# One layer of a graph network: TensorE's increments moved from the last matmul of a group to a drain

## The chip, the core and the metric

The kernel runs on one core of one Trainium2 chip (trn2). A core has five engines with an instruction stream each: PE (TensorE, matmuls), DVE (VectorE), ACT (ScalarE), POOL (GpSimd) and SP (SyncE), and 16 DMA engines that carry what these issue. Engines order themselves by semaphores: an instruction adds one to a semaphore when it is done (`then_inc`), and another engine waits until the semaphore has reached a number (`wait_ge`). The metric is the device time of one execution in microseconds (us); less is better.

## What is computed

6250 nodes have 128 features each, and 206250 edges (sorted by their target node) have 50 features each. In the names of the reference, with x the input and h its normalised copy:

```
h   = relu(layernorm(x))
W   = silu(edge_attr @ fw1 + fb1) @ fw2 + fb2        # a filter for every edge
t   = silu(h @ aw1 + ab1) @ aw2 + ab2                # a row for every node
agg = segment_sum(W * t[src], dst)                   # sums over the edges of a target
out = x + h + silu(agg @ ow1 + ob1) @ ow2 + ob2
```

All of it is in float32, but for the bias fb2, which is split in three bf16 parts that are added by a matmul.

## The kernel before, in words

**First stage.** The rows t of all nodes are computed in seven chunks and written to a table in HBM (`node_table`).

**Edge stage.** The padded edges are cut into 202 pairs of groups; a pair is 1024 edges, a group 512. 196 pairs are "main" pairs and take t[src] from the table; 6 "early" pairs compute it from gathered rows of x. For main pair q the engines do this:
- POOL (L281 to L288) issues 8 indirect DMAs, each of which gathers 128 rows of the table into one of five buffers `xg`. Before the first four of a pair, and again before the last four, it waits on `msg_done`: the buffer must have been consumed by the pair five places before.
- PE has one stream. In `pair(q)` (L769) it does `hidden(q + 1)`: two matmuls of the 50 edge features with fw1, one for each group (`hidden_of`, L738; written to `hid_ps`); then, for each of the two groups, `filters_of` (L745): four matmuls with fw2 and one that adds fb2, into one of four banks `fil_ps`; then `window(q - 2)` (`window_of`, L752): two matmuls that scatter row sums into a window of 64 target nodes.
- ACT does silu on the hidden layer (L353, sets `hid_done`) and multiplies the messages by a mask, eight instructions (L357).
- DVE multiplies filters with gathered rows (`msg`, L595, sets `msg_done`), builds the one-hot matrices (L563, L567), sums rows (L571, sets `red_done`) and adds the window of pair q - 3 to `agg` (L576).

A float32 matmul of the program is two instructions MATMUL and two LDWEIGHTS in the trace, a bf16 one is one of each. So `hidden_of` is 4 + 4 instructions, `filters_of` 9 + 9 and `window_of` 4 + 4; a pair has 26 MATMUL and 26 LDWEIGHTS. Records of some L749 and L742 matmuls are missing in the trace; their weight loads are there.

**Who waits for PE.** `hidden_of` ends with an increment of `hid_sum` (ACT's silu waits for it, and SP's next load of edge features), `filters_of` with one of `fil_done` (DVE's product waits for it, and ACT before it overwrites `hid`), `window_of` with one of `win_done` (DVE's addition). The same three helpers serve the early pairs with semaphores of their own. Transposes (L680) and the layers of the nodes (L686, L691, L698, L795) have their own increments on matmuls.

**Order.** `main_part` (L61) is written out by hand: main pairs come in runs of 32, 32, 32, 32, 32, 20, 8 and 8 (`RUNS`). Between runs stand an early pair (five times, one more before the first run) and the output of nodes whose sums are complete (`output`, L818 on PE). POOL's stream knows no runs: it gathers on until the five buffers are full.

Of the kernel before, what the change touches and what calls it, by code (L numbers as in the profile page):

```python
# [28 lines left out]
WIN = 64  # L29
# [57 lines left out]
def gnn_layer(nc, x, src_t, dst_t, attr_t, fw1, fb1, fw2, fb2, aw1, ab1, aw2, ab2, ow1, ob1, ow2, ob2, out):  # L87
# [8 lines left out]
    with ExitStack() as ctx:  # L96
        def sb(name, shape, dt=f32):
            return ctx.enter_context(nc.sbuf_tensor(name, shape, dt))
# [11 lines left out]
        fw1_s = sb("fw1_s", [P, F])  # L110
# [31 lines left out]
        sums = sb("sums", [P, SETS, 2, F])  # L142
        onehot = sb("onehot", [P, SETS, 2, WIN])
# [25 lines left out]
        hid_ps, fil_ps, sum_ps = bank[0:2], bank[2:6], bank[6:8]  # L169
# [507 lines left out]
        def _(pe):  # L677
# [60 lines left out]
            def hidden_of(to, features, signal):  # L738

                for half in range(2):  # L740
                    at = slice(HALF * half, HALF * half + NG)
                    i = pe.matmul(to[half], fw1_s[at, :], features[at, :], start=True, stop=True)  # L742
                i.then_inc(signal, 1)

            def filters_of(to, b, signal):  # L745
                for j in range(TPG):
                    pe.matmul(to[:, j * P:(j + 1) * P], hid[:, b, j * P:(j + 1) * P], w["fw2_s"][:, :],  # L747
                              start=(j == 0), stop=False)
                pe.matmul(to, ones_b[:, :], fb2_rows[:, :, :].rearrange("p j f -> p (j f)"), start=False,  # L749
                          stop=True).then_inc(signal, 1)  # L750

            def window_of(s, b, signal):  # L752
                for m in range(2):
                    i = pe.matmul(sum_ps[b][:, 0:WIN], sums[:, s, m, :], onehot[:, s, m, :], start=(m == 0), stop=(m == 1))  # L754
                i.then_inc(signal, 1)

            def hidden(q):
                if q % PART == 0:
                    pe.wait_ge(attr_in[q // PART % 2], (q // PART // 2 + 1) * 32)
                pe.wait_ge(hid_done, run(2 * q + 1, 2))  # L760
                at = q % (2 * PART) * GC
                hidden_of(hid_ps, attr[:, at:at + GC], hid_sum)

            def window(q):
                pe.wait_ge(win_added, run(q, 2))
                pe.wait_ge(red_done, run(q))
                window_of(q % SETS, q % 2, win_done)

            def pair(q, s, last):  # L769
                if s == 0:  # L770
                    hidden(q)
                if not last:
                    hidden(q + 1)
                for h in range(2):
                    g = 2 * q + h
                    pe.wait_ge(msg_done, run(g, 4))
                    pe.wait_ge(hid_done, run(g))
                    filters_of(fil_ps[g % 4], g % 4, fil_done)
                if s >= 2:
                    window(q - 2)  # L780
                if last:
                    window(q - 1)
                    window(q)

            def early(r, mlp):
# [10 lines left out]

                pe.wait_ge(e_attr_in, r * 32 + 32)
                hidden_of(e_hid_ps, e_attr, e_hid_sum)
                transposed(0)
                first_layer(0)  # L800
                for h in range(2):
                    e = 2 * r + h
                    pe.wait_ge(e_msg_done, run(e, 1))
                    pe.wait_ge(e_hid_done, run(e))
                    filters_of(e_fil_ps, h, e_fil_done)
                    if h == 0:
                        transposed(1)
                    pe.wait_ge(s_mid, run(mlp + h))
                    pe.wait_ge(s_res, run(mlp + h, 1))
                    layer2(e_l2_ps, TPG, w["aw2_s"][:, :], s_l2)  # L810
                    if h == 0:
                        first_layer(1)
                pe.wait_ge(e_oh_done, r + 1)
                pe.wait_ge(e_red_done, r + 1)
                window_of(0, 0, e_win_done)
                pe.wait_ge(e_added, r + 1)

# [65 lines left out]
```

## Time and profile before

| | |
|---|---|
| time, median of 2 runs | 2673.2 us (2668.84 to 2677.57) |
| the profiled execution | 2694.56 us, of it the span from first to last instruction 2692.7 us |
| busy share of the span | POOL 57%, PE 47%, DVE 45%, PE weight loads 33%, ACT 30% |
| mean granted TensorE clock | 0.669 of full speed |
| DMA | mean 60 GB/s; the gathers (queue q0) 106.01 MB, 15.0% of the 16 engines' time |

A row of a group of instructions gives line, engine and operation, the tiles written and read, and how many (x); then busy time in all, the mean of one in ns, and the time its engine stood idle just before them with what ended that. A row of a timeline begins with start and duration in us; in brackets stands the idle time before it and what ended it. "issue" means that nothing the profile shows was waited for, "remote" that the releaser was not found.

### The profile page before, as it was taken

The numbers are of one execution on the slowest core, as the hardware profiler recorded it, in microseconds if no ns is written. First come the engines' busy times: TensorE is split into PE (matmuls) and PEld (weight loads), VectorE is DVE, ScalarE is ACT, GpSimd is POOL, SyncE is SP. The second block draws the span as 40 slices with busy tenths as digits, with TensorE's granted clock in tenths as the row PEclk, the third lists the DMA queues.
The fourth block names the chain that finished last, engine by engine and source line by source line (L and its number), as shares of the span: only waits on it lengthen the run. The fifth ranks groups of instructions, "written<-read, shape, count | busy, mean of one in ns | idle before, by whom it ended". The sixth has DMA issues, their size and how long they took to land.

```text
span 2692.7 us, 19814 instructions
## 1 busy us (share of the span) xinstructions
PE 1275.5 (47%) x5623; PEld 894.4 (33%) x5727; DVE 1208.9 (45%) x1637; ACT 798.9 (30%) x2154; POOL 1538.6 (57%) x1623
## 2 busy tenths in 40 slices
PE   1344554544544545445445454545444545553544
PEld 1233332332433433323333332333333323332333
DVE  2624444434445443544443444544454443445345
ACT  1222332323323223323332332323232322322232
POOL 7346666626666635666645666654666663666552
PEclk8666666667666656776667677666767667666766
DMA  4212222202222212222212222211222221222210
GB/s 128 93 29 69 56 71 61 68 27 67 62 57 72 59 36 58 71 57 73 57 44 54 65 61 57 73 50 48 58 69 57 72 56 43 54 72 56 55 50 21
DMA packets 64445, 160.54 MB, mean 60 GB/s; under 512 B 28144, under 2 KB 30036, under 8 KB 59436
## 3 DMA queue, kind: packets, MB, share of 16 engines
q0 software_dynamic: 51712, 106.01, 15.0%
q1 hardware_dynamic: 10176, 49.70, 6.9%
q10 hardware_dynamic: 2448, 3.54, 0.4%
q8 instruction: 48, 0.79, 0.1%
q14 instruction: 61, 0.50, 0.1%
HBM read 152.72 MB, written 6.42 MB: 59 GB/s over the span
## 4 chain that ended last, share of the span: by engine, by line
another core or an unknown queue 37%; DVE 23%; PE 20%; issue 14%; DVEq 3%; ACT 3%; DMA 0%; SPq 0%; ACTq 0%
DVE sums L571 12%; PE banks L747 7%; DVE msg L595 6%; PE banks L742 5%; DVEq L574 3%; PE banks L754 2%; PE banks L749 2%; ACT msg L357 1%; DVE onehot L567 1%; PE banks L686 1%; PE banks L698 1%; PE banks L691 1%; DVE agg L576 1%; PE banks L795 1%
## 5 line engine op out<-in xcount | busy, mean ns | idle before, releaser
L286 POOL DMA_INDIRECT xg<-node_table,src x1568 | 1491.3, 951 | 1091.8 <-DVE msg L595 599.6
L357 ACT ACTIVATE msg<-msg,other 128x128 f32<-128x128 f32 x1616 | 494.5, 388 | 1392.5 <-DVE msg L595 1315.5
L595 DVE TENSOR_TENSOR msg<-banks,xg 128x512 f32<-128x512 f32 x392 | 269.5, 688 | 1187.2 <-remote 1033.4
L571 DVE TENSOR_REDUCE sums<-msg 128x128 f32<-128x1024 f32 x404 | 753.1, 1904 | 10.4 <-ACT msg L357 3.5
L747 PE MATMUL banks<-fw_s,hid 128*128 128x128 f32 x3232 | 628.2, 342 | 206.1 <-issue 205.6
L747 PEld LDWEIGHTS banks<-fw_s,hid 128*128 128x128 f32 x3232 | 563.3, 247 | 435.8 <-issue 391.7
L754 PE MATMUL banks<-onehot,sums 128*128 128x64 f32 x808 | 168.4, 347 | 854.8 <-DVE agg L576 471.4
L754 PEld LDWEIGHTS banks<-onehot,sums 128*128 128x128 f32 x808 | 152.2, 258 | 908.4 <-issue 885.7
L742 PE MATMUL banks<-attr,fw_s 50*128 50x512 f32 x784 | 303.9, 862 | 140.0 <-ACT hid L353 116.0
L353 ACT ACTIVATE hid<-banks,cols 128x512 f32<-128x512 f32 x392 | 244.5, 672 | 204.5 <-remote 128.4
L749 PE MATMUL banks<-fb_rows,ones_b 128*128 128x512 bf16 x300 | 139.4, 465 | 33.6 <-issue 33.6
L742 PEld LDWEIGHTS banks<-attr,fw_s 50*128 50x128 f32 x784 | 76.6, 239 | 174.6 <-ACT hid L353 131.2
L329 ACT ACTIVATE mid<-banks,cols 128x512 f32<-128x512 f32 (+4 forms) x28 | 22.9, 817 | 168.6 <-PE banks L686 74.3
L576 DVE TENSOR_TENSOR agg<-agg,banks 128x64 f32 x202 | 42.8, 212 | 52.4 <-issue 22.2
L749 PEld LDWEIGHTS banks<-fb_rows,ones_b 128*128 128x128 bf16 x404 | 47.8, 118 | 55.2 <-issue 55.0
L567 DVE SCALAR_TENSOR_TENSOR onehot<-iota,ends,onehot 128x64 f32<-128x64 f32 x202 | 55.6, 275 | 0.0
L275 POOL DMA_INDIRECT e_x<-in_x,src x48 | 46.0, 959 | 16.1 <-issue 14.3
L691 PE MATMUL banks<-aw_s,mid 128*128 128x128 f32 x194 | 30.0, 310 | 36.0 <-ACT mid L329 36.0
L795 PE MATMUL banks<-hT,aw_s 128*128 128x512 f32 x24 | 22.6, 1043 | 48.0 <-DVE hT L615 47.2
L563 DVE TENSOR_TENSOR onehot<-iota,ends 128x64 f32<-128x64 f32 x202 | 43.7, 216 | 0.0
L691 PEld LDWEIGHTS banks<-aw_s,mid 128*128 128x128 f32 x194 | 28.3, 224 | 38.6 <-ACT mid L329 38.0
L622 DVE TENSOR_TENSOR e_x<-banks,rows 128x512 f32<-128x512 f32 x12 | 8.3, 692 | 72.7 <-PE banks L691 54.7
(89 smaller groups left out, 315.6 us busy)
## 6 DMA issues: line engine op xcount, KB each, us to landing
attr<-in_attr SPq DMA_DIRECT2D x98, 400.0 KB
xg<-node_table,src POOLq DMA_INDIRECT x1568
xs<-in_x SPq DMA_DIRECT2D x5, 448.0 KB
node_table<-res SPq DMA_DIRECT2D x5, 448.0 KB, 2.5
out<-res ACTq DMA_DIRECT2D x5, 448.0 KB, 2.5
e_attr<-in_attr SPq DMA_DIRECT2D x12, 100.0 KB
msg<-in_dst SPq DMA_DIRECT2D x1, 808.0 KB
src<-in_src SPq DMA_DIRECT2D x1, 784.0 KB
```

Source lines behind the costliest of these rows:

```text
L286: pool.indirect_dma_start(xg[:, q % XG, j, :], None, table[:, :], bass.IndirectOffsetOnAxis(ap=src[:, q * L + j:q * L + j + 1], axis=0))\
L353: act.activation(hid[:, g % 4, :], hid_ps[h], ACT.Silu, bias=cols[:, 0:1]).then_inc(hid_done, 1)
L357: i = act.activation(msg[:, b, 1, j, :], msg[:, b, 0, j, :], ACT.Identity, scale=other[:, tiles + j:tiles + j + 1])
L567: dve.scalar_tensor_tensor(out=onehot[:, b, 1, :], in0=iota[:, 0:WIN], scalar=ends[:, 1, q:q + 1], in1=onehot[:, b, 0, :], op0=ALU.is_equa ...
L571: dve.reduce_sum(sums[:, s, m, :], msg[:, b, m, :, :].rearrange("p j f -> p f j"), AX.X).then_inc(signal, 1)
L574: base = dve.value_load(base_i[0:1, q:q + 1], min_val=0, max_val=N_NODES)
L595: dve.tensor_tensor(msg[:, q % 2, 0, tiles, :].rearrange("p j f -> p (j f)"), fil_ps[(2 * q + h) % 4], xg[:, q % XG, tiles, :].rearrange(" ...
L691: i = pe.matmul(to[:, j * P:(j + 1) * P], mid[:, j * P:(j + 1) * P], weights, start=True, stop=True)
L742: i = pe.matmul(to[half], fw1_s[at, :], features[at, :], start=True, stop=True)
L747: pe.matmul(to[:, j * P:(j + 1) * P], hid[:, b, j * P:(j + 1) * P], w["fw2_s"][:, :], start=(j == 0), stop=False)
L749: pe.matmul(to, ones_b[:, :], fb2_rows[:, :, :].rearrange("p j f -> p (j f)"), start=False, stop=True).then_inc(signal, 1)
L754: i = pe.matmul(sum_ps[b][:, 0:WIN], sums[:, s, m, :], onehot[:, s, m, :], start=(m == 0), stop=(m == 1))
```

## The change

At the end of `hidden_of`, `filters_of` and `window_of` the last matmul no longer carries the increment. A `drain` is issued behind it on PE, and the drain carries the increment. The matmuls, their order, all waits and all numbers waited for stay as they are. Increments of the transposes and of the node layers stay on their matmuls.

```
-                    i = pe.matmul(to[half], fw1_s[at, :], features[at, :], start=True, stop=True)
-                i.then_inc(signal, 1)
+                    pe.matmul(to[half], fw1_s[at, :], features[at, :], start=True, stop=True)
+                pe.drain().then_inc(signal, 1)
...
                 pe.matmul(to, ones_b[:, :], fb2_rows[:, :, :].rearrange("p j f -> p (j f)"), start=False,
-                          stop=True).then_inc(signal, 1)
+                          stop=True)
+                pe.drain().then_inc(signal, 1)
...
-                    i = pe.matmul(sum_ps[b][:, 0:WIN], sums[:, s, m, :], onehot[:, s, m, :], start=(m == 0), stop=(m == 1))
-                i.then_inc(signal, 1)
+                    pe.matmul(sum_ps[b][:, 0:WIN], sums[:, s, m, :], onehot[:, s, m, :], start=(m == 0), stop=(m == 1))
+                pe.drain().then_inc(signal, 1)
```

## Rows read from the trace of the kernel before

**Rows 1.** The page's costliest groups of instructions, over the whole span.

```profile
L286 POOL DMA_INDIRECT xg<-node_table,src x1568 | 1491.3, 951 | 1091.8 <-DVE msg L595 599.6
...
L595 DVE TENSOR_TENSOR msg<-banks,xg 128x512 f32<-128x512 f32 x392 | 269.5, 688 | 1187.2 <-remote 1033.4
...
L747 PE MATMUL banks<-fw_s,hid 128*128 128x128 f32 x3232 | 628.2, 342 | 206.1 <-issue 205.6
L747 PEld LDWEIGHTS banks<-fw_s,hid 128*128 128x128 f32 x3232 | 563.3, 247 | 435.8 <-issue 391.7
```

**Rows 2.** Who waited for whom, whole span: us in total, times, longest us.

```profile
DVE msg L595 <- remote: 1033.4, 142, 12.5
...
POOL xg L286 <- DVE msg L595: 599.6, 98, 42.4
```

**Rows 3.** The same for POOL alone, 606 to 1000 us (second run of 32 pairs).

```profile
POOL xg L286 <- DVE msg L595: 53.4, 13, 5.0
```

**Rows 4.** Timeline inside that run, 843 to 873 us.

```profile
843.99 0.68 DVE L595 TENSOR_TENSOR msg<-banks,xg 128x512 f32<-128x512 f32 x1
...
845.27 2.08 PE L747 MATMUL banks<-fw_s,hid 128*128 128x128 f32 x8
...
847.56 1.09 PE L747 MATMUL banks<-fw_s,hid 128*128 128x128 f32 x8
...
850.25 1.16 PE L747 MATMUL banks<-fw_s,hid 128*128 128x128 f32 x8
...
851.47 0.50 PE L747 MATMUL banks<-fw_s,hid 128*128 128x128 f32 x3
...
852.96 0.27 PE L747 MATMUL banks<-fw_s,hid 128*128 128x128 f32 x1 [1.00 <-issue]
...
854.47 0.69 DVE L595 TENSOR_TENSOR msg<-banks,xg 128x512 f32<-128x512 f32 x1 [5.75 <-issue]
...
862.48 0.95 POOL L286 DMA_INDIRECT xg<-node_table,src  x1 [0.30 <-issue]
867.15 0.69 DVE L595 TENSOR_TENSOR msg<-banks,xg 128x512 f32<-128x512 f32 x1 [11.80 <-remote]
...
868.11 0.95 POOL L286 DMA_INDIRECT xg<-node_table,src  x1 [4.68 <-DVE msg L595]
...
871.75 0.69 DVE L595 TENSOR_TENSOR msg<-banks,xg 128x512 f32<-128x512 f32 x1
```

**Rows 5.** Engines by stretch: length, busy us (instructions) of each, clock, DMA share, GB/s.

```profile
192.37:198.54 6.17, 5.16 (x32) 2.90 (x30) 5.34 (x7) 4.68 (x14) 4.73 (x5) 1.00 0.16 43
...
838.72:868.11 29.39, 13.80 (x65) 9.79 (x65) 11.74 (x16) 7.43 (x21) 18.92 (x20) 0.67 0.31 79
605.00:961.00 356.00, 176.22 (x786) 124.61 (x800) 168.09 (x215) 111.07 (x308) 230.60 (x245) 0.66 0.25 64
```

**Rows 6.** Timeline after POOL's restart at 192.37 us.

```profile
200.24 1.27 ACT L353 ACTIVATE hid<-banks,cols 128x512 f32<-128x512 f32 x2 [0.34 <-remote]
...
204.55 0.27 PE L747 MATMUL banks<-fw_s,hid 128*128 128x128 f32 x1 [0.51 <-issue]
```

**Rows 7.** Timeline between the second and third run, 960 to 1018 us.

```profile
960.84 0.69 DVE L595 TENSOR_TENSOR msg<-banks,xg 128x512 f32<-128x512 f32 x1
...
968.28 2.08 PE L742 MATMUL banks<-e_attr,fw_s 50*128 50x512 f32 x4
...
975.26 1.27 ACT L383 ACTIVATE hid<-banks,cols 128x512 f32<-128x512 f32 x2 [9.72 <-remote]
...
1009.66 1.13 PE L742 MATMUL banks<-attr,fw_s 50*128 50x512 f32 x4 [1.18 <-DVE res L642]
1010.84 1.27 ACT L353 ACTIVATE hid<-banks,cols 128x512 f32<-128x512 f32 x2 [5.91 <-PE banks L742]
...
1016.77 0.69 DVE L595 TENSOR_TENSOR msg<-banks,xg 128x512 f32<-128x512 f32 x1 [7.03 <-remote]
...
1017.73 0.94 POOL L286 DMA_INDIRECT xg<-node_table,src  x1 [42.06 <-DVE msg L595]
```

## The prediction

> **What bounds the kernel now.** I read the groups of instructions first. The reader should see that no engine is busy throughout, and that POOL, the busiest, issues 1568 gathers [rows 1]. A gather costs 0.95 us plus 0.30 us between two [rows 4], 1.25 us in all, so a pair costs 10 us and 196 pairs 1960 us: the floor of the edge stage. The waits say what comes on top: POOL stood 599.6 us until a product of DVE freed a buffer [rows 2]. In a run of 32 pairs it waited 53.4 us in 13 pauses [rows 3], 1.67 us a pair, so 327 us over 196 pairs; the remaining 273 us are the eight long pauses between runs, one of which was 42.06 us [rows 7].
>
> The timeline shows what stops DVE in a run. After the product at 843.99, PE issues four groups of filters (845.27, 847.56, 850.25, 851.47) and DVE makes its products in that order: the one at 854.47 uses the first, the one at 867.15 the second, whose matmuls were over by 849 [rows 4]. DVE waited 11.80 us. It was not for gathered rows: POOL had filled all five buffers and could only stop (last gather issued at 862.48), so the oldest of forty had been issued 50 us before. It was for `fil_done`: PE's increment came 18 us after its matmul. Between the products at 854.47 and 867.15 lie 12.68 us, and one filter group is 18 instructions: 0.70 us each. And PE's own issue, eight matmuls in 1.1 us until then, falls to such steps from 852.96. So instructions of PE leave it slowly, increments come out in their order, and once the queue behind is full, issue slows too. The release comes when POOL stops: 3.7 us after its last gather ended at 863.43 comes the product at 867.15, POOL goes on at 868.11, and the next product (871.75) waits for nothing [rows 4]. With gathers under way an early pair's first layer, done by 970.36, was seen by ACT at 975.26; without gathers the same matmuls ended at 1010.79 and ACT began at 1010.84 [rows 7]. This is a loop: PE held, DVE starved, POOL full, POOL stops, PE released.
>
> **How much gets through.** After a restart 32 + 30 instructions of PE go by before the first late one (ACT at 200.24 [rows 5, 6]); its issue has visibly slowed by 204.55 [rows 6]. A cycle from restart to restart (838.72 to 868.11) has 65 + 65 = 130 instructions of PE and 20 gathers, 2.5 pairs [rows 5]. My balance: 62 pass at once (6.2 us); then one per 0.70 us until the release at 28.4 us, 31 more; 130 - 93 = 37 stand in the queue when it opens. For n pairs a cycle, 52n = 62 + (10n - 2.5) / 0.70 + 37, which gives n = 2.5.
>
> **The change, part by part.** Each of 202 first layers, 404 filter groups and 202 windows gets a drain: 808 more instructions on PE, 4 a pair. Removed is nothing but the increment on the matmul.
>
> (a) The drain itself. No row has one. Below I bound it by nothing, above by the 0.70 us steps of rows 4. I take 0.25 us: a weight load of L747 takes 247 ns [rows 1] and no longer overlaps the matmul before it. That is nearest, because the drain's sure effect is that break. In a run that is 1.0 us a pair on PE, which is busy 176.22 of 356 us, 5.5 us of 11.1 a pair [rows 5], so it is hidden by the wait for gathers; without that cover it would cost 196 us. Between runs the chain goes through PE: two windows, then with an early pair its first layer, two filters and window, then first layers and filters of the next run, about nine drains in five gaps and five in three, 60 x 0.25 = +15 us. At 0 us it is 0, at 0.70 us +42.
>
> (b) The wait that the drain adds. Behind it on PE stand the next group's weight loads, which now don't enter the queue until the drain is through; for them wait ACT (silu), DVE (product, window) and so POOL. If a drain waits until the instructions before it have come out, the 37 that now stand in the queue at the release can't be there; at most one group of 18 can. With 56 instructions a pair: 56n = 62 + (10n - 2.5) / 0.70 + 18 gives n = 1.83. A pause costs 1.67 x 2.5 = 4.2 us a cycle; over 1.83 pairs that is 2.29 us a pair, +0.62, x 196 = **+121 us**. Ends: nothing queued, n = 1.40, 3.0 us a pair, +260 us; the whole queue kept, n = 2.28, +0.17, +33 us; below zero only if a drain's increment escapes the hold, which is a rival. I take the middle one, since a group of 18 is what rows 4 show coming out in one piece.
>
> The Trainium skill ("PSUM — Partial Sum Buffer", section "Engine vs sequencer instructions") says that the increment belongs on the matmul, and that a drain waits for the engine to go fully idle. That speaks against this change: it is (b); no row here shows a drain beside matmuls.
>
> (c) The semaphores' other waiters, SP for feature loads among them, see the same order and numbers; SP loads four pairs ahead, so a shift of under 1 us is nothing.
>
> Sum against the profiled execution: 2692.7 + 15 + 121 = 2829, plus the 1.9 around the span, 2831. Its median stands 0.8% below the profiled time (2673.2 / 2694.56 = 0.992), so the forecast is **2808, say 2810 us**. That the unprofiled time is so near also says that the pauses are not made by profiling alone: without them it would be 300 us less.
>
> **Rival 1: the drain's increment escapes (faster).** If the drain waits only for the array and its increment is not queued behind the instructions, and issue no longer clogs, POOL never pauses in a run: 327 less 0.3 for each of some 90 pauses, -300 us. Between runs 56 us pass from last to first product [rows 7], and with empty buffers POOL fills 50 of them: 42.06 becomes some 7, five times -35; two short pauses of together some 34 us vanish. 2692.7 - 300 - 175 - 34 + 15 = 2199, timed 2180. The increments left on matmuls would still be held between runs (4.9 us for one at 975.26), at three or four a gap up to +100: 2280. If only every second pause goes, 2540. For it: the increments are what DVE waits for. Against: PE's issue slows to the same steps for matmuls that carry no increment (852.96), and that a drain can't mend. It decides from the point where a pause comes less often than every four pairs.
> The Trainium skill ("Perfetto Trace Analysis", section "Sequencer-only Instruction (DRAIN, etc)") has a drain's increment pushed by the sequencer and not by the engine, which would be this rival.
>
> **Rival 2: prompt increments, same limit (no change).** The increments escape, but PE's instructions still pass at 0.70 us while gathers run: whole queue kept, +33, drains +15, and an early pair's first layer and filters come sooner, some 7 us in five gaps, -35. 2692.7 + 13 = 2706, timed 2690 (2650 to 2725).
>
> **Rival 3: nothing stays queued and drains are slow.** 2692.7 + 260 + 42 = 2995, timed 2970; if DVE, which then has no filters ready, falls behind after each release by one group's 1.1 to 2.1 us [rows 4], per 1.4 pairs, +150: 3120.
>
> **Chances.** The forecast's case (2730 to 2930) 0.38; rival 3 0.16; rival 2 0.22, of which 0.20 inside 2%; rival 1 0.24. Within 2% (2620 to 2727, about what a measurement tells from no change) 0.20, slower 0.56, faster 0.24. The likeliest case's own range is 2730 to 2930. For 8 in 10 I leave out the full form of rival 1 (0.16) and the tail over 3030 (0.04): 2560 to 3030.
>
> **What would show it.** (b) right: POOL's pauses in a run come every 16 gathers or less instead of 20 and their sum over a run of 32 is above 70 us; filters of at most one group are issued between a held product and its release; the wait of DVE on "remote" stays. (a) right: drains of 0.1 to 0.3 us between runs, the long pauses some 2 us longer each. Wrong, and rival 1 right: few pauses in runs, DVE waiting on gathers that landed just before, long pauses of 7 to 25 us. Rival 2 right: increments within 1 us of the matmul's end and still pauses of 4 us every 2 to 2.5 pairs, with PE issuing in 0.70 us steps ahead of them. If the 0.70 us steps are gone altogether, my account of the queue is wrong.

## The result: slower, and the profile after

The changed kernel takes **2867.48 us** (median of 2 runs, 2859.3 to 2875.66) against 2673.2: a ratio of **1.0727, with a 95% interval of 1.0575 to 1.0878**. The forecast was 2810 us, slower: right in direction, 57 us too low. The profiled execution took 2875.66 us, its span 2873.9 us, 181.2 us more than before, at a mean granted clock of 0.636 (before 0.669).

The page's groups of instructions after the change, in the order of [rows 1]; each helper of the change has moved one line for every line put in, and the product of filters is still L747:

```profile
L286 POOL DMA_INDIRECT xg<-node_table,src x1568 | 1487.6, 949 | 1278.4 <-DVE msg L595 790.8
...
L595 DVE TENSOR_TENSOR msg<-banks,xg 128x512 f32<-128x512 f32 x392 | 270.7, 691 | 1229.2 <-PEq L751 1204.7
...
L747 PE MATMUL banks<-fw_s,hid 128*128 128x128 f32 x3232 | 698.8, 385 | 483.2 <-issue 478.8
```

And who waited for whom, as in [rows 2], over the whole span (us in total, times, longest us), then for POOL alone in the run of 32 pairs that answers to [rows 3] (606 to 1050 us):

```profile
DVE msg L595 <- PEq L751: 1204.7, 324, 11.8
...
POOL xg L286 <- DVE msg L595: 790.8, 107, 48.7
```

```profile
POOL xg L286 <- DVE msg L595: 130.1, 18, 44.7
```

The reader sees the loss in one number. POOL does the same 1488 us of work, but waits 790.8 us for a product of DVE where it waited 599.6 [rows 2]: +191.2 us beside a span that is 181.2 us longer. DVE waits on `PEq L751`, the drain of the filters, 1204.7 us, where the wait of [rows 2] had no releaser's name. In the timelines, eight pauses between runs are over 14 us and add up to 283.4 us (before: eight, 273.9 us); 99 pauses inside runs hold the other 507.4 us (before: 90 pauses, 325.7 us).

One cycle from restart to restart of POOL, the counterpart of [rows 4] and of the window 838.72:868.11 in [rows 5]:

```profile
878.82 0.94 POOL L286 DMA_INDIRECT xg<-node_table,src  x1 [6.63 <-DVE msg L595]
...
882.63 1.13 PE L747 MATMUL banks<-fw_s,hid 128*128 128x128 f32 x8 [0.23 <-issue]
...
888.78 0.69 DVE L595 TENSOR_TENSOR msg<-banks,xg 128x512 f32<-128x512 f32 x1 [2.80 <-PEq L751]
...
888.89 0.63 PE L755 MATMUL banks<-onehot,sums 128*128 128x64 f32 x4 [2.92 <-issue]
...
894.38 2.08 PE L742 MATMUL banks<-attr,fw_s 50*128 50x512 f32 x4 [4.86 <-issue]
895.07 0.22 DVE L576 TENSOR_TENSOR agg<-agg,banks 128x64 f32 x1 [1.88 <-PEq L756]
...
897.54 0.94 POOL L286 DMA_INDIRECT xg<-node_table,src  x1 [0.30 <-issue]
901.34 1.26 ACT L353 ACTIVATE hid<-banks,cols 128x512 f32<-128x512 f32 x2 [9.39 <-PEq L743]
...
901.51 2.05 PE L747 MATMUL banks<-fw_s,hid 128*128 128x128 f32 x8 [5.05 <-issue]
...
903.35 0.63 PE L749 MATMUL banks<-fb_rows,ones_b 128*128 128x512 bf16 x1
904.11 0.69 DVE L595 TENSOR_TENSOR msg<-banks,xg 128x512 f32<-128x512 f32 x1 [8.69 <-PEq L751]
...
905.07 0.94 POOL L286 DMA_INDIRECT xg<-node_table,src  x1 [6.58 <-DVE msg L595]
```

```profile
878.82:905.07 26.25, 11.98 (x54) 7.45 (x54) 11.11 (x14) 7.31 (x20) 15.10 (x16) 0.70 0.15 41
```

Read it from the middle. The window's four matmuls are over by 889.6. The next instruction of PE, the first layer, starts at 894.38: the drain of the window stood between, and DVE, which waits for it, begins at 895.07. The first layer is over by 896.5, but ACT sees it at 901.34 and PE issues the filters at 901.51, 2.9 and 3.0 us after POOL's last gather ended (898.48). In [rows 4] PE issued four groups of filters between the product at 843.99 and the held one at 867.15; here it issues none between the product at 888.78 and the release, and the product at 904.11 has to wait for filters that are not yet computed. So after the release PE must first compute them (901.51 to 904), and POOL waits for that too: 6.58 us, where it waited 4.68. After its stand PE also has the lower clock: from 901.5 to 904 the granted clock was 0.50 and eight of these matmuls took 2.05 us, from 882.6 to 886 it was 1.00 and they took 1.13. The cycle holds 16 gathers, not 20.

The drains themselves, from the views of their two lines (count, then shortest, median and longest in ns, then first and last start in us; the rest of the line can be left aside). A drain's duration runs from its issue, so it includes what the group in front still has to do:

```profile
L751 PEldq DRAIN  x404: 1201/2450/14925, 147.4 to 2852.0; - x135
```

```profile
L743 PEldq DRAIN  x202: 961/2074/8322, 121.6 to 2845.1; - x101
```

### The profile page after: what moved, and what is told of

Read it like the earlier page. It is cut to its first block, busy times and chain, and to the rows that moved or that the text cites. A ratio compares the mean times of both kernels' runs of the same rounds, so it can differ in the third digit from the quotient of the medians.

```text
span 2873.9 us, 20726 instructions
## 1 busy us (share of the span) xinstructions
PE 1493.4 (52%) x5727; PEld 939.7 (33%) x5727; DVE 1226.8 (43%) x1637; ACT 810.4 (28%) x2154; POOL 1534.8 (53%) x1623
## 4 chain that ended last, share of the span: by engine, by line
issue 55%; PEld 23%; PEldq 7%; DVE 5%; PE 5%; another core or an unknown queue 2%; ACT 2%; DVEq 0%; DMA 0%; SPq 0%; ACTq 0%
PEld banks L747 17%; PEld banks L755 3%; PEldq L751 3%; PEld banks L742 2%; DVE sums L571 2%; PEldq L743 2%; PEldq L756 1%; PE banks L686 1%; ACT msg L357 1%; PE banks L698 1%; PE banks L691 1%; PEldq L778 1%; PE banks L796 1%; PE banks L747 1%
## 5 line engine op out<-in xcount | busy, mean ns | idle before, releaser
L286 POOL DMA_INDIRECT xg<-node_table,src x1568 | 1487.6, 949 | 1278.4 <-DVE msg L595 790.8
L747 PE MATMUL banks<-fw_s,hid 128*128 128x128 f32 x3232 | 698.8, 385 | 483.2 <-issue 478.8
L747 PEld LDWEIGHTS banks<-fw_s,hid 128*128 128x128 f32 x3232 | 613.0, 283 | 857.0 <-issue 847.9
L595 DVE TENSOR_TENSOR msg<-banks,xg 128x512 f32<-128x512 f32 x392 | 270.7, 691 | 1229.2 <-PEq L751 1204.7
L742 PE MATMUL banks<-attr,fw_s 50*128 50x512 f32 x784 | 352.7, 990 | 383.0 <-issue 356.9
L755 PEld LDWEIGHTS banks<-onehot,sums 128*128 128x128 f32 x808 | 142.0, 249 | 426.6 <-issue 422.4
L742 PEld LDWEIGHTS banks<-attr,fw_s 50*128 50x128 f32 x784 | 88.5, 270 | 426.0 <-issue 393.9
L749 PE MATMUL banks<-fb_rows,ones_b 128*128 128x512 bf16 x404 | 207.4, 513 | 0.0
L680 PE MATMUL banks<-ident,hs 128*128 128x128 f32 x97 | 19.2, 346 | 51.2 <-issue 51.2
```

Of the source, the lines that this page charges most:

```text
L286: pool.indirect_dma_start(xg[:, q % XG, j, :], None, table[:, :], bass.IndirectOffsetOnAxis(ap=src[:, q * L + j:q * L + j + 1], axis=0))\
L595: dve.tensor_tensor(msg[:, q % 2, 0, tiles, :].rearrange("p j f -> p (j f)"), fil_ps[(2 * q + h) % 4], xg[:, q % XG, tiles, :].rearrange(" ...
```

## The experiments

One thing must be said first: the kernel before itself ran in two ways. In the first comparison and in the two last sets below it took 2673, 2699 and 2686 us; in the two sets between it took 2068.0 and 2066.8 us (31 and 25 runs), and POOL did not pause. Sets of both kinds bear the number of the same chip, so it isn't a property of one chip. I call them "with pauses" and "without pauses", and compare only within a set.

The traces of the two kinds differ in one more way. The view of DMA issues gives for the gathers their count and, where their landings are on record, the median time to landing in us; here for the kernel before (with pauses) and for the changed kernel in a set without pauses:

```profile
xg<-node_table,src POOLq DMA_INDIRECT x1568
```

```profile
xg<-node_table,src POOLq DMA_INDIRECT x1568, 2.5
```

The median is missing in all five gathering kernels traced with pauses and there in all seven without. The packed traces of the five hold 8,586 to 11,154 records of semaphore updates, those of the seven 31,079 to 31,134; some updates of the engines are missing too, not only those of the gathers. In the two kernels below that have direct transfers in place of the gathers, in a set with pauses, the transfers' median is there (2.2 and 2.3 us) and the records number 30,167 and 30,171; only the early pairs' gathers, which are still indirect, have none. So in the traces with pauses a wait "on remote" may be one whose releaser was just not recorded. Every execution that is listed by itself carries a span and a granted clock, so none is known to have run without the profiler's recording, and whether that recording has a part in the pauses was not tested.

### All drains, or one kind, without pauses (before: 2068.01 us)

The three drains alone, with the increments left where they were:

```
                 i.then_inc(signal, 1)          # first layer; the window likewise
+                pe.drain()
...
                           stop=True).then_inc(signal, 1)
+                pe.drain()
```

> The increments stay on the matmuls, and a drain without an increment stands behind each group. If the cost of the change is the wait that a drain puts between groups (my theory), this runs as the changed kernel does: 1.06 to 1.09 of before, POOL pausing every 16 gathers with 5 to 6.6 us. If the cost is that the drain's own increment comes later than the matmul's (rival), it stays near before, 0.99 to 1.02.

Then the change for the filters alone (404 drains), for the window alone and for the first layer alone (202 each):

```
-                          stop=True).then_inc(signal, 1)
+                          stop=True)
+                pe.drain().then_inc(signal, 1)
```

> Drains behind the filter groups alone, 404 of 808. Balance: 54 instructions a pair and at most one group of 18 queued, but a window and a first layer can still be queued behind it: 26 to 34 of the 37. n = 2.1 to 2.3, so +40 to +90 us: 1.015 to 1.035. A rival counts drains: half of them cost half, +95 us, 1.036; another says that each kind of drain stops PE fully, so any one gives the whole cost, 1.07.

> Drains behind the windows alone, 202 of 808, one a pair. A window stands last in PE's order of a pair, so its drain holds up the next pair's first layer and filters: up to 44 instructions that are queued ahead in the kernel before. My theory: +40 to +110 us, 1.015 to 1.04. By the count of drains: +48 us, 1.018.

> Drains behind the first layer alone, 202 of 808. It stands before the filters and holds up 36 instructions of filters. My theory: +30 to +100 us, 1.01 to 1.04, and the same for the window within 30 us. By the count of drains: +48 us, 1.018.

Measured: bare drains 2069.53 us, 1.0012 (1.0002 to 1.0022); filters alone 2067.45, 0.9995 (0.9985 to 1.0004); window alone 2068.99, 1.0004 (0.9994 to 1.0013); first layer alone 2068.7, 1.0004 (0.9994 to 1.0014). Without pauses nothing is left to attribute to one kind of drain: the expectations for each, which took the pauses for granted, could not be tested here.

### The changed kernel again, and more or fewer instructions on PE, without pauses (before: 2066.8 us)

> The changed kernel itself again. In the four runs before this one the kernel before took 2068 us, not 2673, and POOL gathered without a pause. If that holds here, my theory (the cost is made of POOL's pauses, which a held PE causes) expects no difference: within 0.5%, since 4 drains a pair stand beside 10 us of gathers, and between runs POOL has 50 us of free buffers. If the pauses are back, 1.06 to 1.09. A rival in which drains cost time by themselves expects 1.01 to 1.07 also without pauses.

Measured: 2071.36 us, **1.0021 (1.0011 to 1.0031)**. The same program that cost 7.3% cost 0.2%, 4.6 us. POOL's group and its waits in that run, from the view of who waited for whom:

```profile
DVE msg L595 <- DMA xg<-node_table,src: 566.9, 200, 9.3
...
POOL xg L286 <- issue: 471.1, 1546, 0.3
```

DVE now waits for gathered rows, and of POOL's 1568 gathers 1546 have nothing but the 0.3 us of issue before them. The same drains are short:

```profile
L751 PEldq DRAIN  x404: 1168/1468/4083, 92.5 to 2041.4; - x135
```

Two edits ask about the number of PE's instructions, one extra matmul for each half of a first layer (8 instructions a pair more) and the filters' matmuls in bf16 (16 fewer; less exact):

```
                     at = slice(HALF * half, HALF * half + NG)
+                    pe.matmul(to[half][:, 0:1], fw1_s[at, :], features[at, 0:1], start=True, stop=True)
```

```
-        hid = sb("hid", [P, 4, GC])
+        hid = sb("hid", [P, 4, GC], bf16)
...
-                    pe.matmul(to[:, j * P:(j + 1) * P], hid[:, b, j * P:(j + 1) * P], w["fw2_s"][:, :],
+                    pe.matmul(to[:, j * P:(j + 1) * P], hid[:, b, j * P:(j + 1) * P], fw2_b[:, :],
```

> The kernel before with two more matmuls of one column in every first layer (its first column computed twice), 8 more PE instructions a pair and hardly any PE time. With pauses: 60 instructions a pair, n = 95.4 / 45.7 = 2.09, +66 us, 1.025. Without pauses: 1.00.

> The kernel before with the filters' matmuls in bf16 (hidden layer and fw2 rounded, so less exact): 16 fewer PE instructions a pair. With pauses: 36 instructions a pair, n = 95.4 / 21.7 = 4.4, -141 us, 0.947. If held increments are a matter of time after a restart and not of the count of instructions: 1.00. Without pauses: 1.00.

Measured: 2068.3 us, 1.0003 (0.9993 to 1.0013), and 2061.9 us, 0.9975 (0.9965 to 0.9984). PE's busy share fell from 64% (the changed kernel of this set) to 50% with bf16 and brought 5 us: with POOL at its floor of gathers PE does not matter. Neither tells anything on the held queue, which wasn't there. Of the versions that gather, the bf16 one is the only one faster than the kernel before, by a quarter of a per cent and at the price of exactness.

### No gathers, and many matmuls, in a set with pauses (before: 2698.76 us)

Direct transfers in place of the gathers, without and with the change:

```
-                        pool.indirect_dma_start(xg[:, q % XG, j, :], None, table[:, :],
-                                                bass.IndirectOffsetOnAxis(ap=src[:, q * L + j:q * L + j + 1], axis=0))\
-                            .then_inc(gathered[q % XG][h], 16)
+                        first = (q * L + j) % NODE_TILES * P
+                        pool.dma_start(xg[:, q % XG, j, :], table[first:first + P, :]).then_inc(gathered[q % XG][h], 16)
```

> The gathers are replaced by direct transfers of the same size, from consecutive rows of the table instead of the rows that src names (what is left out is the indexing; the output differs). It takes POOL's descriptor work away: POOL needs 1.25 us for each of 8 gathers a window now. If a direct transfer costs POOL's queue 0.1 us or less, POOL's share of 1568 x 1.25 = 1960 us is gone and the bound becomes TensorE (busy two thirds of the run): 1500 to 1900 us. If POOL writes the descriptors of a direct transfer at the same price, 2067 us stays.

> The same direct transfers with all three drains of the change. With POOL's cover away, the drains' own price lies on the path: at 0.1 to 0.3 us for each of 808 it is 80 to 240 us over the run without drains; at 0 (the pipeline empties anyway before the increment is of use) within 20 us of it. If instructions were held behind the transfers as in the first profile, 120 us and more with stalls on the message product.

Measured: **1504.38 us** without drains and **1514.18** with them, 0.5574 and 0.5611 of the kernel before, so the drains cost 9.8 us, 0.65%, inside the 20 us expected of a drain that costs nothing of its own; the mean granted clock was higher with them (0.888 against 0.845), so this is their price less what the clock gave back. The waits of the first, whole span, and a stretch of it with eight transfers under way:

```profile
POOL xg L287 <- DVE msg L594: 492.4, 171, 47.9
...
DVE msg L594 <- remote: 60.0, 8, 8.0
```

```profile
612.81 4.23 POOL L287 DMA_DIRECT2D xg<-node_table  x8 [1.13 <-DVE msg L594]
...
613.55 1.16 PE L746 MATMUL banks<-fw_s,hid 128*128 128x128 f32 x8
...
614.76 1.05 PE L746 MATMUL banks<-fw_s,hid 128*128 128x128 f32 x8
```

In a set in which the kernel before paused, the same bytes moved by direct transfers left PE alone: eight matmuls in 1.16 us beside POOL's queue, and DVE's waits without a releaser fell to 60.0 us from the 1033.4 of [rows 2]. So the bytes alone don't hold PE; with direct transfers the hold isn't there. The two streams differ in their rhythm too: POOL stands some 1.2 us after every eight transfers (4.23 us of issue) here, where the gathers of [rows 4] follow each other for 25 us, and a kernel with direct transfers in an unbroken stream was not run. POOL's waits here are those of an engine that is ahead.

What the drains do to PE in this kernel, in the same two places (first without them, then with them):

```profile
609.20 1.16 PE L746 MATMUL banks<-fw_s,hid 128*128 128x128 f32 x8
...
610.19 1.08 PEld L746 LDWEIGHTS banks<-fw_s,hid 128*128 128x128 f32 x8
```

```profile
610.55 0.97 PEld L746 LDWEIGHTS banks<-fw_s,hid 128*128 128x128 f32 x8 [0.59 <-issue]
610.59 1.13 PE L746 MATMUL banks<-fw_s,hid 128*128 128x128 f32 x8 [0.23 <-issue]
```

The weight loads of the second group followed at once; behind a drain they come 0.59 us after the last load of the group before, and PE stands 0.23 us. DVE, busy 432 of the 500 us from 400 on in both kernels, covers nearly all of that.

Then 20 extra matmuls ahead of the product of each half of a first layer, without and with the change:

```
+                    for _ in range(20):
+                        pe.matmul(to[half][:, 0:1], fw1_s[at, :], features[at, 0:1], start=True, stop=True)
                     i = pe.matmul(to[half], fw1_s[at, :], features[at, :], start=True, stop=True)
```

> The kernel before with 20 more one-column fp32 matmuls ahead of the product of every half of the first layer: 160 more TensorE instructions a pair of windows (they overwrite a column that the real product then writes again, so the output stays). It asks whether TensorE comes to be held when far more of its instructions pass beside POOL's gathers. Held at a limit per instruction (in the first profile 0.70 us each while gathers run, 26 gathers-long stretches between pauses): a pair would issue some 225 instructions, which at 0.70 us is 157 us against POOL's 20 us a pair, so the time would go far above 3000 us with pauses of POOL on DVE's message product. No such limit in this state of the chip: the extra matmuls cost their own time on TensorE, and from the profile of the changed kernel's repeat (TensorE busy 200 of 300 us) some 160 x 0.03 to 0.06 us = 5 to 10 us a pair, of which TensorE's idle third of the time takes up about 6; so 2067 us to at most 2500 us.

> The same 160 extra matmuls a pair, with all three drains of the change. Here TensorE has less slack, so each of the 808 drains should show more of its price. If a drain costs TensorE alone what its emptying takes (0.1 to 0.3 us each) and TensorE has become the bound: 80 to 240 us over the run with the same matmuls and no drain. If TensorE is still covered by POOL: within 10 us of it. If instructions are held: more than 200 us over it, with POOL pausing on the message product.

Measured: **4722.8 us and 5300.14 us**. (The first expectation has three slips: POOL takes 10 us a pair and not 20, a pair has 52 + 160 = 212 instructions and not 225, and the pauses come every 16 to 20 gathers and not 26.) The price of the extra matmuls was wrong: PE was the bound, and each MATMUL of one column with its 128-column LDWEIGHTS took 0.15 to 0.21 us, where I had put 0.03 to 0.06 on an instruction. A time far above 3000 us was what I expected of a hold, but at 0.70 us an instruction a pair would take 148 us, and it took 24. The page's line of the engines, first without and then with drains:

```profile
PE 4381.5 (93%) x21693; PEld 4003.2 (85%) x21887; DVE 1224.6 (26%) x1637; ACT 817.0 (17%) x2154; POOL 1540.3 (33%) x1623
```

```profile
PE 4743.9 (89%) x21693; PEld 4203.9 (79%) x21887; DVE 1223.6 (23%) x1637; ACT 817.8 (15%) x2154; POOL 1542.8 (29%) x1623
```

The spans are 4716.5 and 5302.2 us, 585.7 apart. For the same matmuls PE was busy 362.4 us longer, at a granted clock of 0.552 where it had 0.583, and idle 223.3 us longer: **0.28 us of idle time for each of 808 drains**, the size taken in step (a). The whole difference, 577 us or 0.71 us a drain, is above the 80 to 240 us that I expected with PE as the bound. If busy time went as one over the granted clock, the lower clock would explain some 246 of the 362.4 us (an estimate from the two clocks); why the clock fell and what made the rest is not shown. Whether PE's instructions were also held here isn't settled: POOL gathers for only 10 us at a time, and 42 of PE's weight loads passed in 6.23 us beside gathers:

```profile
2449.22 6.23 PEld L743 LDWEIGHTS banks<-attr,fw_s 50*128 50x128 f32 x42 [0.32 <-issue]
```

### Bare drains once more, with pauses (before: 2685.6 us)

The kernel is that of the first experiment.

> The three drains with the increments left on the last matmul of each group, once more, because in the last set of runs the kernel before took 2699 us again, with POOL's pauses. If it does so here: by the theory that a drain lets no further instruction of TensorE be queued, the drains alone cost what the change cost, 150 to 220 us (ratio 1.055 to 1.08), with pauses of POOL every 16 gathers, although every increment is where it was; by the rival that the increments' new place costs it (they come later than the last matmul's), under 30 us (ratio below 1.01). If the kernel before takes 2067 us here, the run can't tell them apart: 1.001 again.

Measured: **2855.34 us, 1.0627 (1.0601 to 1.0653)**, 170 us more, with every increment still on its matmul. Waits over the span, then the run of pairs from 606 to 1050 us, then the cycle that answers to the one shown above:

```profile
DVE msg L595 <- PE banks L750: 847.7, 229, 10.1
...
POOL xg L286 <- DVE msg L595: 777.8, 104, 47.4
```

```profile
POOL xg L286 <- DVE msg L595: 130.4, 18, 47.4
```

```profile
881.70 0.94 POOL L286 DMA_INDIRECT xg<-node_table,src  x1 [6.65 <-DVE msg L595]
...
893.92 1.08 PE L756 MATMUL banks<-onehot,sums 128*128 128x64 f32 x4 [2.50 <-issue]
...
900.13 2.08 PE L742 MATMUL banks<-attr,fw_s 50*128 50x512 f32 x4 [5.12 <-issue]
...
904.29 1.27 ACT L353 ACTIVATE hid<-banks,cols 128x512 f32<-128x512 f32 x2 [7.31 <-remote]
...
904.47 2.04 PE L748 MATMUL banks<-fw_s,hid 128*128 128x128 f32 x8 [2.27 <-issue]
...
907.05 0.69 DVE L595 TENSOR_TENSOR msg<-banks,xg 128x512 f32<-128x512 f32 x1 [7.29 <-PE banks L750]
...
908.01 0.94 POOL L286 DMA_INDIRECT xg<-node_table,src  x1 [6.64 <-DVE msg L595]
```

It is the changed kernel's cycle: 26.31 us, 16 gathers, a pause of 6.6 us, and PE standing 5.12 us in the drain of the window. The theory that the drain as an instruction costs it, because nothing may queue behind it, expected 1.055 to 1.08; the rival that the increment's new place costs it expected less than 1.01. The rival falls as the main cause. What the new place adds is not resolved: the change cost 194 us and the bare drains 170, in two sets, and the ratio of the first (two runs of each kernel) is known only to 1.0575 to 1.0878.

## Why the prediction was right, and which terms were off

**The direction and the wait were right**, step (b); the size was right in part by luck (below). A drain lets nothing of PE queue behind it, so the stand falls between the groups; the bare drains cost 6.3% by themselves, and the trace shows the stand: 4.9 us before L742 at 894.38. From the window's first matmul to there it is 5.5 us for a group of eight instructions, 5.6 at 0.70 us each; one cycle on, the same stretch (917.96 to 925.66) takes 7.7. The Trainium skill ("PSUM — Partial Sum Buffer", section "Engine vs sequencer instructions") says that a drain waits until the engine is fully idle. The trace agrees: with direct transfers the weight loads behind a drain come 0.59 us after the last one in front of it, where without the drain they follow at once. The same section puts the increment on the matmul, and does so for correctness, because one on a trailing nop can come too early; it allows a drain where a barrier is wanted. It states no price, so it does not by itself speak for or against the 7.3%, and with the increments left on the matmuls the bare drains cost 6.3%.

**How often POOL pauses** was right for the run that it was read from, and not for the rest. In that run 32 pairs had 13 pauses before [rows 3], one for 2.46 pairs; after, the 18 pauses less the long one of 44.7 us make 17, one for 1.88 pairs (forecast 1.83; one for 2.0 in the cycle shown). Over all 196 pairs there were 90 short pauses before and 99 after, one for 2.18 and one for 1.98 pairs: the cycle of 2.5 pairs in rows 5 was longer than the average one, which I had not counted. The balance raised the number of pauses by 37% (from one in 2.5 pairs to one in 1.83); over the span it rose by 10%.

**How long a pause is** was the term that failed. Step (b) kept "4.2 us a cycle", as before. Measured over the span, it was 325.7 / 90 = 3.6 us before and 507.4 / 99 = 5.1 us after. The filters that used to stand ready in the banks at the release are now computed after it. I had named this, DVE without filters ready, and put it under rival 3 as an extra of one group's 1.1 to 2.1 us; it belonged into the forecast. Of the 181.7 us that pauses inside runs grew by, 99 x (5.12 - 3.62) = 149 us is their length and 9 x 3.62 = 33 us their number. The forecast put all of its +121 us on the number and nothing on the length: the two errors, 88 us too much and 149 too little, partly cancel, and that the sum came near is so far luck. In all step (b) is short by 61 us. The gaps between runs give 6 back (next point) and the rest of the span 10, which leaves the 45 us by which the sum missed the profiled execution (2831 against 2875.66).

**Step (a)** forecast +15 us in the gaps between runs; the eight long pauses grew by 9.5 us together, but one by one they changed by -5.7 to +6.6 us, so that sum is no measure of a drain, and the sign I had given, some 2 us longer each, is not seen. The 0.25 us of a drain is the 0.28 us of idle time measured where PE is the bound, and hidden where POOL is (4.6 us for 808 drains). I had said 196 us if the cover were gone. It depends on what else is there: 9.8 us when DVE carries the chain, 577 us when PE does, where the matmuls got longer as well, at a lower granted clock.

**The signs.** Pauses every 16 gathers: seen. More than 70 us in a run of 32: 85.4 (130.1 less the long pause). At most one group issued between a held product and its release: only the window and the first layer, and of filters none. DVE's wait with no releaser's name did not stay, it moved to the drain's name.

**Rival 1** falls: the increment does not escape. The first layer was over by 896.5, ACT saw its drain's increment at 901.34, and DVE's product waited for drains for 1204.7 us in all. The rule of the Trainium skill that a drain's increment is pushed by the sequencer ("Perfetto Trace Analysis", section "Sequencer-only Instruction (DRAIN, etc)") isn't contradicted, the waits bear PE's sequencer as their releaser. It does not help: the increment came when the instructions in front were through. **Rival 2** falls with it. **Rival 3** had part of the truth, the longer pause, but 2.0 pairs a cycle and not 1.40.

**What I took for fixed and is not** is that PE is held at all. With no pauses the whole of (b) is gone and the ratio is 1.002. The range of 2560 to 3030 us holds no case for it. What starts the held queue stays open. Shown is that it isn't there when direct transfers take the place of the gathers in a set with pauses. Not shown is why the same kernel has it in some sets of runs and not in others, nor by which path gathers slow PE. The profiler's recording, which loses records of gathers in the sets with pauses alone, is a rival that no run tests, and the prediction's argument against it (an unprofiled time within 0.8% of the profiled one) doesn't hold, since no execution is known to be without it. That PE's instructions leave at 0.70 us each is an argument from two places of one trace, where groups after the change give 0.7 to 1.0, and no experiment reached it.

## What to carry to other kernels

A drain is cheap to look at and dear where it stops run-ahead: here 0.2% where another engine was the bound, 0.28 us of idle TensorE each where TensorE was (and 12% of the time in all), and 7% where the engine's queued instructions were what bridged a stall. Keep increments on the last matmul, and before pricing any wait on an engine ask what that engine does ahead of time now and who lives on it. Where a pause is predicted, ask not only how often it comes but what must be redone between release and restart.

## What the runs showed of the hardware

- The same kernel took 2067 to 2068 us or 2673 to 2699 us, steady within a set (at most 0.4% either way from the median), with a granted clock of 0.66 to 0.67 with pauses and 0.72 to 0.73 without.
- A drain of TensorE lasts as long as what is in front of it: at the least 1.2 us behind a group of filters, 8.3 us at most behind a first layer of eight instructions with pauses (2.1 without). Behind a first layer with 40 extra matmuls it was 5465 ns every time, shorter than the group, which fits a drain that is issued while the end of the group still stands in the queue:

```profile
L745 PEldq DRAIN  x202: 5465/5465/5465, 167.1 to 5267.6; - x101
```

- Gathers cost POOL 0.95 us and 0.30 us between two in every run; a direct transfer of the same 64 KB costs its queue 0.54 us.
- A MATMUL of one float32 column with its 128-column LDWEIGHTS is not small: 42 took 6.3 us in one stretch (0.15 us each, granted clock 0.72) and 8.7 us in another (0.21 us each, granted clock 0.50).
